# An LSTM with a residual: the pieces of w_h are issued from ScalarE's DMA queue

## The reference

```python
xW = jnp.einsum('ntd,dk->tnk', x, Wx) + b       # x is (4, 512, 256), Wx (256, 1024)
def step(carry, xw_t):
    prev_h, prev_c = carry                      # h0 = cond (4, 256), c0 = 0
    a = xw_t + prev_h @ Wh                      # Wh (256, 1024)
    i, f, o = (sigmoid(a[:, k * 256:(k + 1) * 256]) for k in range(3))
    g = tanh(a[:, 768:])
    next_c = f * prev_c + i * g
    next_h = o * tanh(next_c)
    return (next_h, next_c), next_h
out = x + transpose(hs, (1, 0, 2))              # all 512 hidden states, float32
```

## Time and profile before

| | |
|---|---|
| median of 3 runs | 1062.12 us (1061.99 to 1062.6) |
| the profiled execution's own time | 1062.23 us |
| its span, first to last instruction | 1060.4 us |
| mean granted TensorE clock | 0.999 |
| TensorE matmul / VectorE / ScalarE busy | 82% / 74% / 52% |
| bytes on SyncE's queue (q1) / ScalarE's (q10) | 8.41 MB / 0.14 MB |

### The profile page before, as it was taken

One profiled execution on the slowest core, in us unless ns is written; L12 is line 12 of the kernel. 1 busy time (PEld: TensorE's weight loads), 2 busy tenths in 40 slices (PEclk: granted clock), 3 DMA queues, 4 the chain that ended last, 5 costly groups with the idle time before them and its releaser, 6 DMA issues.

```text
span 1060.4 us, 90187 instructions
## 1 busy us (share of the span) xinstructions
PE 867.7 (82%) x37888; PEld 635.6 (60%) x37888; DVE 784.5 (74%) x4899; ACT 548.2 (52%) x3586; POOL 0.7 (0%) x6
## 2 busy tenths in 40 slices
PE   4888888888888888888888888888888888888886
PEld 3666656656666666556566666665665666666654
DVE  5777777777777777777777777777777777777776
ACT  2555555555555555555555555555555555555554
POOL 0000000000000000000000000000000000000000
PEclk9999999999999999999999999999999999999999
DMA  3000000000000000000000000000000000000000
GB/s 91 6 7 6 6 6 6 7 6 6 7 6 6 7 6 6 6 6 7 6 6 7 6 6 6 6 6 6 6 7 6 6 7 6 6 6 6 6 6 7
DMA packets 32110, 8.74 MB, mean 8 GB/s; under 512 B 31584, under 2 KB 31584, under 8 KB 32096
## 3 DMA queue, kind: packets, MB, share of 16 engines
q1 hardware_dynamic: 31488, 8.41, 3.6%
q10 hardware_dynamic: 608, 0.14, 0.1%
HBM read 6.43 MB, written 2.10 MB: 8 GB/s over the span
## 4 chain that ended last, share of the span: by engine, by line
DVE 52%; PE 23%; ACT 15%; issue 8%; SPq 1%; DVEq 1%; DMA 0%
DVE turned_bank L299 40%; PE gates L372 23%; ACT tanh_o L213 8%; DVE h_pad L317 8%; ACT turned_bank L216 6%; DVE scan_both L304 3%; DVEq L333 1%; SPq L140 1%; DVE h_rows L273 0%; DMA wh_raw<-in_L_cond_Wh_dram 0%; SPq L144 0%; PE x_acc L364 0%; PE gates L358 0%; DVEq L272 0%; DVE wh L226 0%
## 5 line engine op out<-in xcount | busy, mean ns | idle before, releaser
L372 PE MATMUL gates<-wh,h_pad 128*32 128x64 f32 x32768 | 565.0, 221 | 175.7 <-DVE h_pad L317 174.2
L372 PEld LDWEIGHTS gates<-wh,h_pad 128*32 128x32 f32 x32768 | 482.6, 110 | 356.3 <-DVE h_pad L317 354.3
L299 DVE STREAM_TRANSPOSE turned_bank<-gates 128x64 f32<-128x64 f32 x2048 | 475.3, 263 | 163.3 <-PE gates L372 153.8
L204 ACT ACTIVATE tanh_f<-turned_bank 128x8 f32<-128x8 f32 x512 | 90.7, 177 | 431.1 <-DVE turned_bank L299 390.5
L364 PE MATMUL x_acc<-wh,zeros 128*32 128x256 f32 x1024 | 305.0, 379 | 0.3 <-issue 0.3
L349 PE MATMUL x_acc<-wx,x_units 128*32 128x128 f32 x2048 | 203.6, 284 | 9.4 <-DVE x_units L252 9.4
L211 ACT ACTIVATE scan_both<-turned_bank 128x8 f32<-128x8 f32 x1024 | 185.1, 181 | 48.5 <-DVE turned_bank L299 1.7
L317 DVE SCALAR_TENSOR_TENSOR h_pad<-tanh_o,turned_bank 128x4 f32<-128x4 f32 x1024 | 133.0, 158 | 73.3 <-ACT turned_bank L216 0.4
L310 DVE TENSOR_TENSOR_SCAN cell<-scan_both 128x12 f32<-128x12 f32 x1024 | 145.2, 182 | 0.0
L216 ACT ACTIVATE turned_bank<-cell 128x4 f32<-128x4 f32 x1024 | 143.7, 173 | 0.0
L349 PEld LDWEIGHTS x_acc<-wx,x_units 128*32 128x32 f32 x2048 | 94.9, 109 | 51.8 <-issue 9.3
(11 more groups left out here) (28 smaller groups left out, 9.1 us busy)
## 6 DMA issues: line engine op xcount, KB each, us to landing
x_next<-in_x_dram SPq DMA_DIRECT2D x256, 8.0 KB
x_here<-in_x_dram SPq DMA_DIRECT2D x256, 8.0 KB
out_dram<-y_rows SPq DMA_DIRECT2D x256, 8.0 KB
wx_raw<-in_L_cond_Wx_dram SPq DMA_DIRECT2D x8, 128.0 KB, 3.4
wh_raw<-in_L_cond_Wh_dram SPq DMA_DIRECT2D x8, 128.0 KB, 2.8
bias_raw<-in_L_cond_b_dram ACTq DMA_DIRECT2D x4, 32.0 KB, 3.0
h_rows<-in_cond_dram ACTq DMA_DIRECT2D x4, 1.0 KB
```

The source lines that it names most:

```text
L299: nc.vector.transpose(turned[k], gates[k][:, 0:W]).then_inc(gates_turned[k], 1)
L372: last = nc.tensor.matmul(gates[k][q * R:(q + 1) * R, 0:W], h_stationary(b, t), wh[:, b, q, columns_of(k)], start=False, stop=b == M - 1, ...
```

## The change

The eight issues of w_h leave SyncE's program and stand in ScalarE's, behind the four of bias and the four of h0, and ahead of the probe activation. The helper that issues them now takes the queue as an argument. What is loaded, where to, and the semaphores are as before.

```diff
+        def load_weights(queue, raw, w, loaded):
+            for b in range(M):
+                for q in range(Q):
+                    at = q * QD + b * R
+                    queue.dma_start(raw[q * R:(q + 1) * R, b, :], w[at:at + R, :]).then_inc(loaded[b], DMA)
+
         @block.sync
         def _(sp):
-            def load_weights(raw, w, loaded):
...
-            load_weights(wx_raw, w_x, wx_loaded)
+            load_weights(sp, wx_raw, w_x, wx_loaded)
             for q in range(Q):
                 sp.dma_start(x_next[q * R:(q + 1) * R, :], x_quadrant(x, 0, q)).then_inc(x_next_loaded, DMA)
-            load_weights(wh_raw, w_h, wh_loaded)
...
                 act.dma_start(h0_rows[q * R:q * R + N, :], cond[:, q * QD:(q + 1) * QD]).then_inc(h0_loaded, DMA)
 
+            load_weights(act, wh_raw, w_h, wh_loaded)
             nc.scalar.activation(table_probe[:, 1:2], table_probe[:, 0:1], ACT.Tanh)
             act.wait_ge(zeroed, 2)
```

## The result

| | before | after |
|---|---|---|
| median of 22 runs each | 1061.69 us | 1063.71 us |
| lowest to highest | 1059.38 to 1062.88 | 1062.44 to 1064.74 |
| ratio | | 1.0023 (95% interval 1.0016 to 1.0029) |
| profiled execution, its span | 1062.23, 1060.4 | 1063.33, 1061.5 |

The change makes the kernel slower by 2.0 us, 0.23%. The forecast was 1060.8 us, which is 1.3 us faster than the median of 1062.12 that was known then. The longer series puts the kernel before at 1061.69. (In the kernel after, lines lie one further up: L371 is the earlier trace rows's L372, L298 is L299.)

The account below looks back on a forecast made before the run. The serial recurrence was taken to bound the kernel, with only the start movable: first recurrent matmul from 15.36 to about 14.05 us, ScalarE and clock at nothing, so 1062.12 - 1.3 = 1060.8 us. Range 1059.5 to 1062.3.

Parts of the forecast that it names:

- What bounds the kernel: Whole kernel: the serial recurrence of 512 steps; the change can move only the start, within SyncE's DMA queue's 1%.
- The ScalarE part: Start, ScalarE's queue: eight w_h issues take 3.68 us, table load moves to 7.92, cover over 4 us; cost nothing.
- The contention bound: Start: two queues with large pieces share the DMA engines; gain from 0.33 us (strict turns) to 2.29 us (no contention).
- Most: Start: strict turns, no more bytes per second; x_next lands at 10.9, first recurrent matmul at 15.03, gain 0.33 us.
- S: Start: the new time of the first recurrent matmul, 15.36 us before, forecast at about 14.05.
- Rival B: Start: x_next takes w_h's place as the wait; S 14.9 to 15.5, time 1061.7 to 1062.3 us; chance 0.13.
- The middle that I took: Start: S about 14.05, between the bounds 13.07 and 15.03, a gain of 1.31 us.
- The row with bias: Start, 2.0 to 2.5 us: w_x at 80% and bias at 28% of engines' time; neither waits for the other's backlog.
- Counted as nothing: SyncE's queue: x_next of chunk 1 and x_here issued earlier, 64 KB; no cost, or 0.1 us lost among w_h pieces.
- What leaves SyncE: SyncE's queue: eight w_h issues, 3.68 us, are gone; x_next of chunk 1 is issued at about 9.2 instead of 11.31.
- Rival C: Start: x_next served behind all of w_h, landing at 12.1, S 16.2, 0.9 us slower, 1063.0 us; chance 0.04.
- The clock: TensorE, 1.2 to 2.4 GHz at about 20 us: no net effect; 0.35 us given back or 0.75 won possible.

Follow-up runs that it names:

- e3: The kernel after with eight tiny 64 B loads in SyncE's program where the w_h issues stood: 1061.98 us, 1.0011 of the kernel before.
- e4: The kernel before with SyncE's wait for the y_rows store moved to x_here's last piece, x_next issued about 1.3 us sooner: 1062.36 us, ratio 1.0004.
- e5: The kernel after with SyncE's wait for the y_rows store moved to x_here's last piece, so x_next is issued sooner: 1061.88 us, 1.0003 of before.
- e10: The kernel after with three already satisfied waits ahead of x_next's issues in SyncE's loop: 1060.18 us, 0.9983 of the kernel before.
- e12: The kernel before with three already satisfied waits ahead of x_next's issues in SyncE's loop, weights as before: 1059.91 us, ratio 0.9985.

## Why the prediction was wrong

- **What bounds the kernel** was right for the start: it was the chain of issues and w_h's landing, and both are gone after.
- **The ScalarE part** was right in kind. The issues took 4.56 us instead of 3.68 and the table load came at 8.83, under cover of 6 us.
- **W**, the landing of the last block of w_x, was inside its bounds: 8.44, between 7.84 and 9.34. w_h, put at 12.15 without contention, landed at 12.93 and was not what the start waited for.
- **The contention bound failed.** "Most" was x_next at 10.9 and S = 15.03; measured 11.46 and 15.58. x_next was given three turns of 0.53 us, and it got its bytes through only by 10.5 us, where three such turns had put them at 10.0. Rival B, S = 14.9 to 15.5, describes what the start does, and S came out just beyond its end. The middle that I took, 14.05, was 1.53 us short of the 15.58 measured. The row with bias was no guide to small pieces behind a full engine.
- **"Counted as nothing" failed, and it is the larger error.** Under "What leaves SyncE", I looked only at who waits for what stood behind the eight issues, and "The change touches nothing in the loop" and "From there on the same 2.01 us steps" took the loop for fixed. That the eight were gone cost 1.0 us in the loop and 0.7 in the tail: with eight tiny loads in their place both went back (e3). 1.5 + 1.0 + 0.7 = 3.2 us is nearly the whole of the 3.3 between a gain of 1.3 and a loss of 2.0.
- **Rival C** named the right sign by the wrong mechanism: x_next was not behind all of w_h, and the start alone costs 0.2 us.
- **The clock** gave one slow step fewer in this trace, within what I had left open.

That DMA landings hold up TensorE's update is shown as far as this: its lateness goes and comes with the time of x_next's landings (49 to 60 ns always, 77 to 109 mixed, 173 and more never, in fifteen traces), follows them to other steps (e4, e5), doesn't depend on what shifted them (e10, e12), and is never seen without landings (none of 14,509). By what path the one delays the other stays open. Within a run the moment of a late update follows SyncE's third issue of x_next more closely than the first landing (after: spread of 5.5 ns against 14, standard deviation), and this is not explained. Open too is why the landings come 40 ns sooner when SyncE's loop lies four or eight instructions further to the front. What is seen, before against after: SyncE begins the first issue of x_next 25 ns sooner behind its last one of x_here, and that issue is 12 ns shorter (709 instead of 721), so that the second follows at 907 ns instead of 918. And the runs of the kernel before spread over 3.5 us, most others over 1.4 to 2.4; its two traces (0.7 us of clock, 0.35 of loop) do not explain that.

## What to carry to other kernels

- A transfer issued earlier on another queue is paid for by what the engines were about to move. Before the move, look for the small, urgent transfer that would stand behind it; try the large pieces one behind the other on one queue, and the small ones on the other. Here that brought the first recurrent matmul 0.6 to 1.5 us forward, where the change of this document put it back by 0.2.
- When a loop has hundreds of short steps, a change outside it can move it. Compare the lengths of start, loop and tail one by one before a difference of 0.2% is laid to the edit, and try the same edit with the program's length kept.
- A DMA that lands beside a critical semaphore update can be shifted by a few instructions for nothing; here that was worth 1.9 us (e12), more than the best start was. A shift moves every landing of the loop, so look at the other updates too.

## What the hardware showed that was not expected

- A semaphore update of TensorE came 60 to 80 ns late in every chunk when a DMA's landing updates began 140 to 150 ns ahead of the time it was due (49 to 60 against 200), in a part of the chunks at 90 to 120 ns ahead, and in none at 10 to 30 ns ahead. In all seventeen traces together 3,453 of 28,660 updates were late, none of them without a landing in the 300 ns before.
- The code's place counts: with eight DMA instructions fewer ahead of the last stores, the last load of code (8 KB) began 3.8 us behind the last h_rows instead of 1.5 us ahead of it. The issuing of the stores was 0.4 us longer and the tail 0.7.
- Two queues with 128 KB pieces moved 258 GB/s together and shared it 0.78 to 0.76 MB; one alone had 234. Beside a full queue, four pieces of 8 KB landed at 11.46 us instead of 8.94.
